# Output weights as the moving operand: VW made with keys on partitions, 26 leftover tokens as float32 in four column tiles

## The reference

```
Q = x @ Wq;  K = ctx @ Wk;  V = ctx @ Wv            # 8 heads of 512
attn = softmax(mask(Q K^T / sqrt(512)))             # over 77 keys
out = (attn @ V, heads side by side) @ Wo + x
return (out - mean) * rsqrt(var + 1e-5) * gamma + beta
```

## Time and profile before

| | us |
|---|---|
| median of 3 runs (lowest to highest) | 352.82 (352.49 to 353.0) |
| the profiled execution | 353.7 |
| its span, first to last instruction | 351.9 |
| PE busy | 346.0 |
| DVE busy | 288.0 |
| ACT busy | 243.7 |
| POOL busy | 213.3 |

### The profile page before, as it was taken

How to read it: one execution, slowest core, us unless ns; L and a number is a source line. 1 busy time by engine, 2 the same in 40 slices (tenths; PEclk the granted TensorE clock), 3 DMA queues, 4 the chain that set the end, 5 groups by cost and what they waited for, 6 DMA issues and landing times. The chain is left out here.

```text
span 351.9 us, 6894 instructions
## 1 busy us (share of the span) xinstructions
PE 346.0 (98%) x2272; PEld 322.0 (92%) x2272; DVE 288.0 (82%) x532; ACT 243.7 (69%) x797; POOL 213.3 (61%) x218
## 2 busy tenths in 40 slices
PE   9999999999999999999999999999999999999994
PEld 6999999999999999998899899889988998899884
DVE  2149999999778768898797988988987989889896
ACT  2268766645777669887886976968778769768560
POOL 0044654400447968689769688687796796885243
PEclk9999999999999999999999999999999999999999
DMA  7998769775635080053142341440532423413012
GB/s 229 423 420 323 280 223 324 281 276 218 221 137 212 0 275 29 1 179 113 68 171 75 116 151 59 152 151 31 181 95 85 152 72 138 149 41 111 32 44 107
DMA packets 19683, 55.81 MB, mean 159 GB/s; under 512 B 1728, under 2 KB 3264, under 8 KB 17728
## 3 DMA queue, kind: packets, MB, share of 16 engines
q1 hardware_dynamic: 18784, 54.38, 42.6%
q10 hardware_dynamic: 864, 1.00, 0.8%
HBM read 46.98 MB, written 8.39 MB: 157 GB/s over the span
## 5 line engine op out<-in xcount | busy, mean ns | idle before, releaser
L1489 POOL TENSOR_TENSOR w_proj_lo<-w_proj,w_proj_hi 128x768 fp32r<-128x768 f32 x20 | 36.9, 1868 | 73.1 <-ACT w_proj_hi L828 73.1
L737 PE MATMUL pair<-vw_hi,pt_hi 128*128 128x512 f32 x155 | 62.1, 400 | 0.0
L737 PE MATMUL pair<-vw_lo,pt_hi 128*128 128x512 f32 x155 | 60.9, 393 | 0.0
L737 PE MATMUL pair<-vw_hi,pt_lo 128*128 128x512 f32 x155 | 60.7, 392 | 0.0
L1438 POOL TENSOR_TENSOR out_sb<-centred,beta_sb 128x512 f32<-128x512 f32 x30 | 38.8, 1295 | 28.8 <-ACT centred L939 28.7
L894 ACT ACTIVATE prob<-c,neg_max 128x77 f32<-128x77 f32 x128 | 43.9, 347 | 0.0
L1483 POOL TENSOR_TENSOR xo_lo<-x_sum,xo_hi 128x512 fp32r<-128x512 f32 x32 | 41.5, 1301 | 0.2 <-ACT xo_hi L918 0.2
L538 PE MATMUL pair<-kv_t,w_out_hi 128*128 128x304 f32 (+1 forms) x160 | 41.6, 334 | 0.0
L661 PE MATMUL pair<-a_hi,xo_hi 128*128 128x304 f32 x128 | 40.0, 313 | 0.0
L661 PE MATMUL pair<-a_lo,xo_hi 128*128 128x304 f32 x128 | 38.6, 302 | 0.0
L661 PE MATMUL pair<-a_hi,xo_lo 128*128 128x304 f32 x128 | 38.6, 301 | 0.0
(11 more groups left out here) (129 smaller groups left out, 1022.3 us busy)
## 6 DMA issues: line engine op xcount, KB each, us to landing
w_out<-wo SPq DMA_DIRECT2D x8, 1024.0 KB, 4.8
xt_in<-x_tiles SPq DMA_DIRECT2D x16, 512.0 KB, 4.0
x_in<-x_rows SPq DMA_DIRECT2D x16, 512.0 KB, 4.7
out<-out_sb SPq DMA_DIRECT2D x31, 256.0 KB, 2.1
w_out<-wq_t SPq DMA_DIRECT2D x7, 1024.0 KB, 8.1
w_proj<-wv SPq DMA_DIRECT2D x8, 768.0 KB, 4.7
w_proj<-wk SPq DMA_DIRECT2D x6, 768.0 KB, 9.9
w_out<-wq_t SPq DMA_DIRECT2D x2, 512.0 KB, 8.2
```

The source lines that it names most:

```text
L737: mm = pe.matmul(ps_out[:, i % 2, 0:s.model], ps[:, j, :], v[:, j, b, :], start=(j == 0 and n == 0), stop=(j == s.key_t - 1 and n == len(p ...
L1489: pool.tensor_tensor(half_cols(w_proj_lo[u % W_RING], half), half_cols(w_proj_sb[u % W_RING], half), half_cols(w_proj_hi[u % 2], half).bit ...
```

## The change

The values of the tokens become the stationary operand and the output weights the moving one, so that VW comes out with keys on partitions and needs no transposes. A stationary tile has 128 columns: 64 tokens of each batch, which are the last 64 of one and the first 64 of the other, since odd heads project a context with the batches swapped (`ctx_turned`, copied by POOL at the start) and the tokens taken are columns 13 to 140 of 154 (`value_product`: four contraction tiles, three passes, 12 matmuls of 512 columns). The 26 tokens left (13 of each batch) are summed to float32 by POOL (`v_rest`, padded to 32) and multiplied in plain float32 in four column tiles of 32 columns, one for each 128 model columns (`value_strips`: 16 matmuls of 128 columns). ACT copies these strips to SBUF, and eight DMAs of 13x128 for each head, 64 in all, on SP's queue, place them in `rest_rows` (`move_strips`). When all are there, ACT and DVE split them into the fifth block of VW (`split_rest`).

With that, every values use projects in plain float32 and splits its values (DVE, `split_kv`) and its output weights: ACT rounds, POOL takes the rest in uses 8 to 13, DVE in 14 and 15. The T sums keep their place. `normalise` writes the 13-token ends of each head to `prob_rest` apart from the 64-token middles, so that the keys stand in VW's new order: one DVE instruction becomes two.

```diff
-    SPLIT_VALUES = (H, *range(H + 4, USES - 1))
-    FULL_VALUES = (H + 2, H + 3, H + 4)
+    RESTS_OF_VECTOR = (USES - 2, USES - 1)
+    STRIPS = P // STRIP
...
+        ps_vw = [ps_outp[0][:, n, 0:s.model] for n in range(2)]
+        ps_strips = [ps_outp[1][:, n, 0:P] for n in range(2)]
...
         def whole(u):
-            return u < FULL_PROJ or u in FULL_VALUES
+            return u < FULL_PROJ or u >= H
         def whole_out(u):
-            return u < FULL_OUT or (u >= H and u not in SPLIT_VALUES)
+            return u < FULL_OUT
...
+            def move_strips(h):
+                sp.wait_ge(act_strip, h + 1)
+                for g in range(STRIPS):
+                    for n in range(s.batches):
+                        b = (h + n) % 2
+                        to, at = place(h, b) * s.rest, g * STRIP + n * s.rest
+                        sp.dma_start(rest_rows[to:to + s.rest, b, g * P:(g + 1) * P],
+                                     strip_sb[h % 2][at:at + s.rest, :]).then_inc(ld_rest[h % 2], DMA_INC)
...
                 load_w_out(u)
+                if u >= H + W_RING:
+                    move_strips(u - H - W_RING)
...
             for c in range(XT_RING):
                 load_xt(c)
+            for h in range(H - W_RING, H):
+                move_strips(h)
...
+            def value_product(u):
+                h = u - H
+                hi, lo = wide(w_out_hi[u % 2]), wide(values_lo(u))
+                wait_kv(u, 1)
+                if u == USES - 1:
+                    open_bank_a()
+                if h == 0:
+                    pe.wait_ge(dve_a_lo, 2 * H)
+                elif h >= 2:
+                    pe.wait_ge(dve_vw_lo, 2 * (h - 1))
+                for k in range(s.dim_t):
+                    if k % 2 == 0:
+                        pe.wait_ge(act_o_hi, 2 * split_before(u) + k // 2 + 1)
+                        pe.wait_ge(dve_o_lo if by_vector(u) else pool_o_lo,
+                                   rests_before(u, by_vector(u)) + k // 2 + 1)
+                    passes = [(0, hi), (0, lo), (1, hi)]
+                    for n, (low, w) in enumerate(passes):
+                        mm = pe.matmul(ps_vw[h % 2], values(u, k, low), w[:, k, :], start=(k == 0 and n == 0),
+                                       stop=(k == s.dim_t - 1 and n == len(passes) - 1))
+                mm.then_inc(pe_outp, 1)
+            def value_strips(u):
+                h, w = u - H, wide(w_out_sb[u % W_RING])
+                pe.wait_ge(pool_v_rest, h + 1)
...
+                for k in range(s.dim_t):
+                    for g in range(STRIPS):
+                        mm = pe.matmul(ps_strips[h % 2][g * STRIP:(g + 1) * STRIP, :], v_rest[u % 2][:, k, :],
+                                       w[:, k, g * P:(g + 1) * P], start=(k == 0), stop=(k == s.dim_t - 1))
+                mm.then_inc(pe_outp, 1)
...
-                if p == 0:
-                    transpose_vw(H)
-                    pe.wait_ge(dve_vw_lo, sum(len(part) for part in plan[:H]))
...
+            def split_rest():
+                for n in range(2):
+                    act.wait_ge(ld_rest[n], DMA_INC * STRIPS * s.batches * (H // 2))
+                act.wait_ge(dve_pad, 2)
+                for b in range(s.batches):
+                    act.activation(vw_hi[0:s.rest_rows, s.key_t - 1, b, :], rest_rows[0:s.rest_rows, b, :], ACT.Copy)\
                        .then_inc(act_vw_hi, 1)
...
             add_u2(0)
-            split_vw(H, [0])
+            split_rest(0)
             add_w2(0)
...
+            for u in range(H, USES):
+                if not by_vector(u):
+                    for half in range(2):
+                        pool.wait_ge(act_o_hi, 2 * split_before(u) + half + 1)
+                        pool.tensor_tensor(half_cols(values_lo(u), half), half_cols(w_out_sb[u % W_RING], half),
+                                           half_cols(w_out_hi[u % 2], half).bitcast(F32), ALU.subtract)\
+                            .then_inc(pool_o_lo, 1)
+                pool.wait_ge(dve_kv_lo, 2 * split_before(u) + 2)
+                if u >= H + 2:
+                    pool.wait_ge(pe_outp, 2 * (u - 1))
+                pool.tensor_tensor(v_rest[u % 2][:, :, 0:s.rest_toks].rearrange("p m (n k) -> p m n k", n=2),
+                                   rest_values(u, 0), rest_values(u, 1), ALU.add)\
+                    .then_inc(pool_v_rest, 1)
```

More of the change, by code:

```diff
@@ L61, in __init__ @@
         self.slot = self.keys + self.keys % 2
+        self.main = P // self.batches
+        self.rest = self.keys - self.main
+        self.rest_toks = self.batches * self.rest
+        self.rest_rows = self.heads * self.rest
         self.key_t = -(-self.row // P)
@@ L65, in __init__ @@
         assert 2 * self.toks <= BANK and self.model <= BANK and self.dim_t == self.model_t == 4
+        assert 0 < self.rest_toks <= STRIP and self.rest_rows <= P and self.heads * self.main == (self.key_t - 1) * P
         assert self.batches == 2 and self.kept % 2 == 0 and self.heads // 2 * self.slot <= BANK
[L68 to L82, removed]
 def build(nc, x_tiles, x_rows, ctx_t, wk, wq_t, wv, wo, mask, gamma, beta, out):
@@ L198, in build @@
         c12 = sb("c12", [P, s.half])
-        sb("gap2", [P, 288])
+        with ExitStack() as early:
+            strip_sb = [early.enter_context(nc.sbuf_tensor(f"strip_sb{n}", [P, P], F32)) for n in range(2)]
+        prob_rest = [sb(f"prob_rest{n}", [P, s.rest_rows]) for n in range(2)]
+        sb("gap2", [P, 288 - 2 * s.rest_rows])
         prob1 = sb("prob1", [P, s.row])
@@ L550, in wait_kv @@
             def wait_kv(u, half):
-                if summed_kv(u):
-                    pe.wait_ge(dve_kv_sum, 2 * sum(summed_kv(v) for v in range(u)) + half + 1)
-                elif whole_out(u):
+                if whole_out(u):
                     pe.wait_ge(act_kv_hi, 2 * u + half + 1)
@@ L570, in project_full @@
                         wait_kv(u - 1, half)
-                    if m == 2 and u > H + 1:
-                        pe.wait_ge(dve_vw_lo, sum(len(part) for part in plan[:u - 1 - H]))
                     mm = full_product(ps_proj[half], m % 2, w_proj_sb[u % W_RING], ctx_of(u), m, s.ctx_t)
@@ L987, in _ @@
             round_sums(1)
-            split_vw(H)
+            split_rest()
             exps_first(0)
@@ L1071, in split_kv @@
             def split_kv(u):
-                if u > H and not whole(u):
-                    dve.wait_ge(dve_t_lo, t_no[T2, 1])
                 for half in range(2):
@@ L1091, in split_kv @@
                        .then_inc(dve_kv_lo, 1)
-            def add_kv(u):
-                for half in range(2):
-                    values = value_of(u)[:, 2 * half:2 * half + 2, :]
-                    dve.wait_ge(act_kv_hi, 2 * u + half + 1)
-                    dve.tensor_tensor(values, second(ps_proj[half], u), values, ALU.add).then_inc(dve_kv_sum, 1)
             def take_out_product(u, half):
@@ L1329, in _ @@
                     take_out_product(u, 0)
-                    if not whole_out(u + 1):
+                    if not whole_out(u + 1) and by_vector(u + 1):
                         split_w_out(u + 1)
```

263 lines of the change are left out of this document (131 added, 132 removed).

## The result

The changed kernel takes 377.88 us (median of 4 runs, 377.4 to 378.28), the kernel before 352.91 beside it (352.49 to 353.11): 1.071 times, interval 1.069 to 1.073. The forecast was 370, a move of +17.6; it is +25.0. The last row is TensorE's granted clock in 40 slices, in tenths of full speed.

The account below looks back on a forecast made before the run. PE, busy 98%, and DVE, 82%, were taken to bound the kernel together. Values stage +11.2, join +4.7 and clock +1.7 gave +17.6 us, so 370 us as median, range 366 to 375 (chance 0.55).

Parts of the forecast that it names:

- The sign: Whole kernel: slower, by +17.6 us; slower had chance 0.84, same 0.05, faster 0.11.
- column tiles in series: Rival, values stage: column tiles run one after another, 2.49 us more a head, about 381 us in sum; chance 0.14.
- Strips 1.0 us, side by side: Values stage on PE: a head's sixteen float32 strip matmuls take 1.0 us, four column tiles sharing the array.
- The product 2.77 us: Values stage on PE: the 12 matmuls of value_product, 512 columns at 0.23 us each, take 2.77 us.
- The paper gain of the values stage: Values stage if PE waited for nothing: 52.1 us, ending at 117.7 in place of 123.5, -5.8 us.
- Turns of DVE and POOL (steps 1 to 3): Values stage: two-SBUF-input instructions alternate, T sums end at 89.95, PE idles 10.6 then 6.0 us before projections 11 and 12.
- The clock, 1.7: PE after the three long waits: half clock costs up to 1.7 us each; one counted, +1.7 us.
- SP has eight more issues ... so nothing: SP's queue, values stage: eight more issues a head at 0.45 us, 3.6 us, delay weight loads harmlessly: no cost.
- the lower bound: Join of the stages: issues of 0.1 us and 1.7 us to land would make its cost +2 us.
- The wait for w2, 4.75: Join: PE's sixth product waits 4.75 us for DVE's w2 sum behind split_rest(0); whole join +4.7 us.
- The main loop, nothing: Main loop: normalise's extra instruction, some 0.15 us a tile, fits DVE's 2 us of slack in 13.8: no cost.
- faster: Rival: PE's saved work decides, if T sums don't stand still for POOL and placement is cheap; 345 to 352 us; chance 0.11.

Follow-up runs that it names:

- run 5: Changed kernel with strips of all four column tiles on partitions 0 to 31, loop turned inside out, two 13x512 placements a head: 378.57 us, 1.072 of the kernel before.
- run 10: run 6 and run 9 together, with DVE's mask_bias also ahead of the memsets and use 14's VW split: 355.69 us, 1.008 of the kernel before.
- run 7: Changed kernel with POOL's twelve subtractions splitting w_out in uses 8 to 13 replaced by memsets writing zeros: 365.02 us, 1.033 of the kernel before.
- run 6: Changed kernel with run 1 and run 2 together, prob_rest in its own gap, more x loads ahead of late strips: 368.74 us, 1.043 of the kernel before.
- run 1: Changed kernel with the first two xt_in loads ahead of the strips of use 12 in SP's queue: 374.28 us, 1.060 of the kernel before.
- run 3: Changed kernel issuing only one of each head's eight placements, rest rows made from the last strips: 368.82 us, 1.045 of the kernel before.
- run 2: Changed kernel with ACT's and DVE's rest-row work behind the first exponentials and first block of transposed probabilities: 376.83 us, 1.067 of the kernel before.
- Run 12: run 10 with 16-row placements, small prob_rest memsets, use 14's strips ahead of SP's wait, ACT rounding x blocks before rest rows: 352.41 us, 0.9987 of the kernel before.
- run 11: run 6 and run 7 together, with DVE's mask_bias also ahead of the memsets and use 14's VW split: 356.54 us, 1.010 of the kernel before.
- run 9: Changed kernel with plain float32 value products in uses 9 to 11, no splits of w_out by ACT and POOL or of values there: 364.27 us, 1.032 of the kernel before.

## Why the prediction was right, and where its terms were off

The sign, the two places and the mechanisms held; the move was 7.4 us too small. At 377.9 the time lies outside the 366 to 375 to which the forecast gave 0.55, and next to the 378 to 384 of the column tiles in series, which is not what happened. In the join, the issues in SP's queue are the step that failed. Step by step:

- **Strips 1.0 us, side by side.** 1.01 from start to start (108.67 to 109.68), and 3.68 in series: run 5. The serial rival is dead. The estimate of 1.1 from the figure for three tiles in the Trainium skill (TensorE: Matmul & The Clock Gate, "Measured speedup vs the span model") was near too: it took 3.2 times for four tiles, and the runs show 3.68 / 1.08 = 3.4.
- **The product 2.77 us.** It is 112.83 to 115.82 = 2.99 us: its first and last matmuls are followed 0.1 us later than the others (0.34 and 0.32 instead of 0.23). Eight of these make 1.8 us that the sum left out. Here the trace may agree with the other rule that the prediction cites from the Trainium skill, that a change of tiling drains the engine (TensorEngine Tiling (Array Packing), "Key Properties"); the gap of the first matmul stands where the tiling stays and 154 columns give way to 512, so the rule isn't shown by it. The paper gain of the values stage is 4.0 and not 5.8 us. Run 10 checks it: from the projection of use 9 at 64.96 its stage takes 121.46 - 64.96 = 56.5 us, less 0.35 of wait and 1.9 for three plain uses 54.2, where it took 123.52 - 65.48 = 58.0 before: 3.8 less.
- **Turns of DVE and POOL (steps 1 to 3).** Shown by run 7. The T sums end at 87.8 instead of 89.95. From 69.55 on they lose 7.0 us to POOL and not 10.3, since the forecast let every turn cost a full instruction; the 1.4 us of the VW split among them, which keeps its time beside POOL, it left out. The idle times are 8.80 and 3.74, not 10.6 and 6.0: 4.1 us less, of which 1.5 is the slow projection that filled the second.
- **The clock, 1.7.** This term was mis-sized by its count. The projections behind the two waits took 4.65 and 4.79 us in place of 3.14, +3.2. In the join 26.33 - 3.50 - 6.12 = 16.7 us remain for work that run 6 does in 150.04 - 135.06 - 2.12 = 12.9: +3.9. Together 7 against 1.7; none of the four waits was without it. The forecast took its price from the warm-up, and 1.7 for a wait was near, but it let only one wait pay. These three terms make E, the end of the last strips: waits 12.5, clock 3.2, content -4.0, sum 11.7 as measured. It agrees with the forecast of 11.2 by luck: there it was waits and POOL's second half 17.0, clock 0, content -5.8.
- **"SP has eight more issues ... so nothing", 0.45 each.** This is the step that failed. An issue takes 0.74 us, and 0.79 to 0.92 from one to the next; the price of a load was no bound for it, nor was the 0.1 us of the lower bound, which no run shows (0.51 is the shortest). And the step asked only what the issues do to the loads of weights, though the order on SP has `xt_in` behind them. The landing of `xt_in` at 128.3 holds ACT and the strips of use 14, so that two heads and not one are still to be placed when the last strips end: the queue is done at E + 12.6 and not at E + 5.6. The first product waits 3.50 and not 0.7. Of these 2.8 us runs 1 and 3 take away 1.4; the other 1.4 is `seed`, which DVE's memsets and `mask_bias` hold longer than the 0.7 allowed. With `mask_bias` moved ahead (run 10) this wait is gone.
- **The wait for w2, 4.75.** The mechanism is right: 6.12, from DVE's `split_rest(0)` behind the DMAs. Runs 2 and 6 remove it, run 3 leaves 1.36. The sixth product starts at E + 15.6 and not at E + 9.8; the wait is only 1.4 longer because the first product and the slow clock take up the rest. The join is +12.8 instead of +4.7: 2.8 for the first product, 1.4 for this wait, 3.9 for the clock.
- **The main loop, nothing.** 214.97 against 214.88.

The rival "faster" named the right condition, T sums that don't stand still and a cheap placement, but no run made the issues as cheap as its -2.1 wanted. Run 12 came near to it another way, with issues of 0.59 us out of the way of the loads: -0.5 in the median. What stays open is why a transfer of 13 or 16 rows inside SBUF holds the queue longer than a load of 128 rows from memory, and what part of the 0.1 us at each end of the product is the tiling.

## What to carry to other kernels

When work goes to an engine because it was idle there, look at what its neighbour does in those microseconds: POOL's 2.4 us for half a weight tensor cost DVE 2.1 us in an instruction of 0.8. Price a DMA by rows of its own kind, count its issues, and write down every load behind it in the queue, with what waits for that load. A wait on TensorE has a second price: each of the four here, whether 3.5 or 8.8 us long, cost 1.5 us or more of slow clock on top. And two repairs that each look small alone (runs 1 and 2) can be one repair, since a wait uncovered is often the one that comes next.

## What the runs showed of the hardware

- The granted clock fell to 0.50 behind all of PE's waits of 3.5 us and more (here 3.50, 3.74, 6.12 and 8.80). Between 2.0 and 3.3 us the length does not decide: it fell behind 2.01 (run 11), 2.12 (run 1) and 2.83 us (run 2), and it stayed at 1.00 behind 2.02 (run 7), 2.20 (run 3), 3.06 (run 2) and 3.27 us (run 9), and behind 2.12 us in run 6, as here:

```profile
139.00:141.00 2.00, 2.00 (x17) 2.00 (x15) 1.17 (x3) 0.75 (x2) 2.00 (x3) 1.00 0.20 62
```

- A DMA issue within SBUF holds SP 0.59 us with 16 rows of 128 columns and 0.74 with 13, 0.75 with 13 rows of 512; a load of output weights 0.33.
- Four float32 column tiles of 32 columns are 3.4 times as fast side by side (1.08) as at one place (3.68).
- POOL's memsets beside DVE's sums cost DVE nothing (792 ns); POOL's two-input instructions cost a sum up to 2.06 us, and cost DVE's split of VW, with one input in PSUM, nothing (0.70 us).
